# A decoder layer on one core: the recurrence of batches 2 and 3 moved into the FFN stage, with five shared PSUM banks and three tile sets

## The reference

```
x = layernorm(x + attention(x, Wqkv, bqkv, Wo, bo))        # 16 heads of 32
x = layernorm(x + wkv(w, u, k=x, v=ctx))                   # a recurrence over the 512 tokens
x = layernorm(x + ffn(x))                                  # 512 -> 2048 -> 512
# wkv: per step t, y = (A*p + E*v)/(A*q + E), then p, q, o are decayed by w and updated
# ffn: Wg = (gate_w - 128)*gate_scale, same for up and down
#      y = (silu(x Wg') * (x Wu')) Wd'
```

## Time and profile before

| | us |
|---|---|
| median of three runs | 837.01 |
| the profiled execution | 835.81 |
| its span (first to last instruction) | 834.0 |
| PE busy in the span | 743.1 |
| DVE busy | 558.8 |
| ACT busy | 408.3 |
| POOL busy | 271.2 |

### The profile page before, as it was taken

One profiled execution on the slowest core, in us unless ns is written; L12 is line 12 of the kernel. 1 busy time (PEld: TensorE's weight loads), 2 busy tenths in 40 slices (PEclk: granted clock), 3 DMA queues, 4 the chain that ended last, 5 costly groups with the idle time before them and its releaser, 6 DMA issues.

```text
span 834.0 us, 11936 instructions
## 1 busy us (share of the span) xinstructions
PE 743.1 (89%) x4256; PEld 404.1 (48%) x4256; DVE 558.8 (67%) x1217; ACT 408.3 (49%) x1000; POOL 271.2 (33%) x284
## 2 busy tenths in 40 slices
PE   5988699978889978999677598889999999999997
PEld 2555456644456545565443254434454444444443
DVE  4455545778998879998898488874774544344434
ACT  5568767777567776686846213302332034104310
POOL 2001233328341155500346515541622133103320
PEclk9999799998999989999979899999999999999999
DMA  7246494232034122141620610001000100010001
GB/s 248 62 138 217 139 215 127 89 114 65 13 89 139 44 72 77 33 117 56 133 44 1 101 51 1 1 13 39 2 1 13 38 1 1 14 38 1 1 13 38
DMA packets 44331, 54.17 MB, mean 65 GB/s; under 512 B 4720, under 2 KB 33648, under 8 KB 44272
## 3 DMA queue, kind: packets, MB, share of 16 engines
q1 hardware_dynamic: 41008, 47.11, 18.0%
q0 software_dynamic: 3264, 6.29, 4.4%
HBM read 47.10 MB, written 12.58 MB: 72 GB/s over the span
## 4 chain that ended last, share of the span: by engine, by line
PE 59%; DVE 18%; issue 6%; POOL 6%; ACT 5%; DMA 3%; SPq 3%; POOLq 0%; DVEq 0%; ACTq 0%
PE psb L717 20%; PE psb L607 7%; PE psb L730 6%; PE psb L728 6%; PE psb L697 5%; PE psb L654 4%; DVE ek L1034 4%; DVE ee L946 3%; PE psb L621 2%; SPq L1270 2%; PE psb L643 2%; DMA xt<-in_xT 2%; PE psb L665 2%; PE psb L704 1%; PE psb L633 1%
## 5 line engine op out<-in xcount | busy, mean ns | idle before, releaser
L946 DVE CUSTOM_DVE_ANT_0 ee<-psb,mask,clip 128x512 f32<-128x512 f32 (+3 forms) x256 | 131.0, 530 | 54.7 <-PE psb L643 54.1
L810 ACT ACTIVATE ee<-ee,nm 128x512 f32<-128x512 f32 (+3 forms) x256 | 142.8, 559 | 32.4 <-DVE nm L946 32.1
L654 PE MATMUL psb<-ident,ee 128*128 128x128 f32 x640 | 108.5, 288 | 25.9 <-ACT ee L821 25.7
L821 ACT ACTIVATE ee<-psb 128x512 f32<-128x512 f32 (+1 forms) x192 | 100.0, 521 | 56.4 <-PE psb L654 56.1
L1212 POOL TENSOR_TENSOR hl<-hf,hh 128x512 f16<-128x512 f32 x64 | 77.5, 1211 | 134.9 <-ACT hh L884 134.9
L884 ACT ACTIVATE hh<-hf 128x512 bf16<-128x512 f32 x64 | 40.4, 632 | 144.1 <-DVE hf L1059 144.1
L717 PE MATMUL psb<-x2h,wg 128*128 128x512 f16 x256 | 99.5, 389 | 6.6 <-DVE th L1049 5.9
L654 PEld LDWEIGHTS psb<-ident,ee 128*128 128x128 f32 x640 | 76.3, 147 | 54.2 <-ACT ee L821 34.5
L717 PE MATMUL psb<-x2l,wg 128*128 128x512 f16 x256 | 99.7, 390 | 0.0
L730 PE MATMUL psb<-wd,hl 128*128 128x512 f16 x256 | 97.0, 379 | 2.3 <-POOL hl L1212 2.3
L717 PE MATMUL psb<-x2h,wu 128*128 128x512 f16 x256 | 97.5, 381 | 0.0
(11 more groups left out here) (106 smaller groups left out, 1236.3 us busy)
## 6 DMA issues: line engine op xcount, KB each, us to landing
qs<-parts SPq DMA_DIRECT2D x64, 128.0 KB, 2.7
ks<-parts SPq DMA_DIRECT2D x64, 128.0 KB, 2.9
parts<-qhl SPq DMA_DIRECT2D x16, 256.0 KB, 2.1
parts<-khl SPq DMA_DIRECT2D x16, 256.0 KB, 2.1
x<-in_x SPq DMA_DIRECT2D x4, 1024.0 KB, 7.8
ct<-in_ctxT SPq DMA_DIRECT2D x4, 1024.0 KB, 6.2
out<-x SPq DMA_DIRECT2D x16, 256.0 KB, 2.0
xt<-in_xT SPq DMA_DIRECT2D x14, 256.0 KB, 4.0
```

The source lines that it names most:

```text
L654: mm = e.transpose(PSB[:, bk, o:o + P], E[H % 3][:, EOFF[i] + j * P:EOFF[i] + (j + 1) * P], IDENT[:])
L810: e.activation(dst, dst, ACT.Exp, bias=NM[:, n % 4, col:col + 1], scale=-1.0, accum_out=DEN[:, n % 4, col:col + 1]).then_inc(sem("exp"), 1)
L821: e.activation(ET[h][:, base:base + width], PSB[:, bank["turn", H, item], 0:width], ACT.Copy).then_inc(sem("et"), 1)
L946: e.tensor_tensor_reduce(E[H % 3][:, EOFF[i]:EOFF[i] + w], PSB[:, bank["score", H, i], 0:w], MASK[:, S - w:S], -SC, CLIP[:, i:i + 1], ALU. ...
```

## The change

Of the recurrence of batch 2, three pieces go from attention groups 14 and 15 to iterations 4, 11 and 14 of FFN batch 0, the fourth to iteration 1 of batch 1. Batch 3's four go to iterations 8, 12 and 15 of batch 1 and 2 of batch 2. `yt` of batch 2 moves to iterations 4 to 7 of batch 1, `yt` of batch 3 to 6 to 9 of batch 2; the load of the context for batch 3 follows `yt` of batch 2 as before. Batch 3's Wo comes after iterations 5 to 8 of batch 0 instead of ahead of iteration 4. The zero-point pass of the down weights stands in iterations 8 to 15 instead of 4 to 11, `x2t` in 12 to 15 instead of 10 to 13. Gate and up take the bank of banks 0 to 4 that is emptied first in the list, and `th`/`hf` tiles come in three sets from iteration 4 on (two before).

```diff
-X2IT, YTIT = (10, 11, 12, 13), (6, 7, 8, 9)
+X2IT, WOIT = (12, 13, 14, 15), 5
+WKV2, WKV3 = ((0, 4), (0, 11), (0, 14), (1, 1)), ((1, 8), (1, 12), (1, 15), (2, 2))
+YT2, YT3 = [(1, 4 + t) for t in range(4)], [(2, 6 + t) for t in range(4)]
+FBANK = (0, 1, 2, 3, 4)
...
-        for u in gu_parts(b, it, ((0, 2), (1, 3))):
+        for u in gu_parts(b, it, (FBANK, FBANK)):
...
-        for c, (g, slot) in enumerate(WKVS):
-            at(m + g, slot, "wkv", b, c)
         if b < B - 2:
+            for c, (g, slot) in enumerate(WKVS):
+                at(m + g, slot, "wkv", b, c)
...
-    wk3 = [lambda c=c: wkv(B - 1, c) for c in range(T)]
-    for it in range(IT):
-        if it >= EARLY:
-            gu(0, it)
+    ffn = {}
+    for c in range(T):
+        ffn.setdefault(WKV2[c], []).append(lambda c=c: wkv(2, c))
+        ffn.setdefault(WKV3[c], []).append(lambda c=c: wkv(3, c))
+        ffn.setdefault(YT2[c], []).append(lambda c=c: yt(2, c))
+        ffn.setdefault(YT3[c], []).append(lambda c=c: yt(3, c))
+        for b in (1, 2, 3):
+            ffn.setdefault((b - 1, X2IT[c]), []).append(lambda b=b, c=c: x2t(b, c))
+    for it in range(EARLY, IT):
+        gu(0, it)
         tick()
-        if it < 4:
-            for u in wo3[3 * it:3 * it + 3]:
+        if it - WOIT in range(T):
+            for u in wo3[3 * (it - WOIT):][:3]:
                 u()
-            tick()
-            yt(B - 2, it)
-        if it in (5, 9, 13):
-            wk3.pop(0)()
-        if 4 <= it < 12:
-            add("zero", "wd", 2 * it - 8)
-            add("zero", "wd", 2 * it - 7)
-        if it in X2IT:
-            x2t(1, X2IT.index(it))
+        if it >= 8:
+            add("zero", "wd", 2 * it - 16)
+            add("zero", "wd", 2 * it - 15)
+        for u in ffn.get((0, it), ()):
+            u()
         tick()
...
                 gu(b, it)
                 tick()
-                if b == 1 and it == 1:
-                    wk3.pop(0)()
+                for u in ffn.get((b, it), ()):
+                    u()
                 tick()
-                if b == 1 and it in YTIT:
-                    yt(B - 1, YTIT.index(it))
-                if b + 1 < B and it in X2IT:
-                    x2t(b + 1, X2IT.index(it))
...
+    def ring(b, it):
+        z = b * IT + it
+        return RINGS[z % 2 if z < EARLY else (z - EARLY) % 3]
+    def ring_had(b, it):
+        z = b * IT + it
+        return max([k + 1 for k in range(z) if ring(0, k) is ring(b, it)], default=0)
...
-            if z >= 2:
-                act.wait_ge(sem("hf"), z - 1)
+            if ring_had(b, it):
+                act.wait_ge(sem("hf"), ring_had(b, it))
```

More of the change, by code:

```diff
@@ L502, in build @@
         wg = sb(f, "wg", [P, T, I], F16)
-        TH, HF = sb(f, "th", [P, 2, S], F32), sb(f, "hf", [P, 2, S], F32)
+        RINGS = [(sb(f, f"th{k}", [P, S], F32), sb(f, f"hf{k}", [P, S], F32)) for k in (0, 1)]
         wd = sb(f, "wd", [P, IT, D], F16)
@@ L506, in build @@
         HS = [(sb(f, f"hh{it}", [P, S], BF16), sb(f, f"hl{it}", [P, S], F16)) for it in range(IT)]
-        sb(f, "pad1", [P, 19 * 256], F32)
+        sb(f, "pad1", [P, 15 * 256], F32)
+        RINGS.append((sb(f, "th2", [P, S], F32), sb(f, "hf2", [P, S], F32)))
         YS = sb(f, "ys", [P, 2, D], F32)
@@ L867, in th @@
         def th(b, it):
-            z = b * IT + it
             act.wait_ge(*by("gate", b, it))
             act.wait_ge(sem("small"), 4)
-            if z >= 2:
-                act.wait_ge(sem("hf"), z - 1)
-            e.activation(TH[:, it % 2, :], PSB[:, bank["gate", b, it], :], ACT.Tanh,
+            if ring_had(b, it):
+                act.wait_ge(sem("hf"), ring_had(b, it))
+            e.activation(ring(b, it)[0][:], PSB[:, bank["gate", b, it], :], ACT.Tanh,
                          scale=GT[:, it:it + 1]).then_inc(sem("th"), 1)
@@ L883, in hh @@
                 act.wait_ge(*by("et", NHG - 1, 2))
-            e.activation(HS[it][0][:], HF[:, it % 2, :], ACT.Copy).then_inc(sem("hh"), 1)
+            e.activation(HS[it][0][:], ring(b, it)[1][:], ACT.Copy).then_inc(sem("hh"), 1)
         for name, *a in tt.order:
@@ L1048, in aa @@
             dve.wait_ge(*by("th", b, it))
-            e.scalar_tensor_tensor(out=TH[:, it % 2, :], in0=TH[:, it % 2, :], scalar=1.0,
+            th = ring(b, it)[0]
+            e.scalar_tensor_tensor(out=th[:], in0=th[:], scalar=1.0,
                                    in1=PSB[:, bank["gate", b, it], :], op0=ALU.add,
@@ L1053, in hf @@
         def hf(b, it):
-            z = b * IT + it
+            th, half = ring(b, it)
             dve.wait_ge(*by("aa", b, it))
             dve.wait_ge(*by("up", b, it))
-            if z >= 2:
-                dve.wait_ge(sem("hl"), z - 1)
-            e.scalar_tensor_tensor(out=HF[:, it % 2, :], in0=TH[:, it % 2, :], scalar=CC[:, it:it + 1],
+            if ring_had(b, it):
+                dve.wait_ge(sem("hl"), ring_had(b, it))
+            e.scalar_tensor_tensor(out=half[:], in0=th[:], scalar=CC[:, it:it + 1],
                                    in1=PSB[:, bank["up", b, it], :], op0=ALU.mult, op1=ALU.mult).then_inc(sem("hf"), 1)
@@ L1211, in hl @@
             pool.wait_ge(*by("hh", b, it))
-            e.tensor_tensor(HS[it][1][:], HF[:, it % 2, :], HS[it][0][:], ALU.subtract).then_inc(sem("hl"), 1)
+            e.tensor_tensor(HS[it][1][:], ring(b, it)[1][:], HS[it][0][:], ALU.subtract).then_inc(sem("hl"), 1)
         e.memset(NT[:], -10000.0).then_inc(sem("nt"), 1)
```

## The result

The changed kernel takes 846.95 us (median of 4 runs, 842.85 to 849.13) against 836.87 for the kernel before: 10.1 us slower, ratio 1.0116, 95% interval 1.0073 to 1.0159. The forecast was 816.7. In its profiled execution the span is 847.3 us against 834.0.

The account below looks back on a forecast made before the run. DVE was taken to bound groups 14 and 15 through batch 2's recurrence, PE the FFN stage. Gains of 15.5 us (attention) and 4.8 (FFN, 16.8 less 12.0) sum to 20.3: 837.0 to 816.7 us, range 806 to 828.

Parts of the forecast that it names:

- The first y product: FFN batch 0: hl(0, 15) as late as before, behind an exp on ACT waiting for `y2`; loss 2.0 us (0 to 4).
- Attention groups: Without recurrence, group 14 gains 3.5 us, group 15 5.4 and 5.1, the finish 1.5; sum 15.5, between about 7 and 19.
- The loads' cost: Group 14: gate weights' loads go out together near 398 us beside re-stacking of group 15's score inputs; 0, at worst 3.
- Rival (a): Attention groups are paced by their chain, gaining 7.5 us instead of 15.5: 824.7 us; chance 0.17.
- ol: FFN batch 0: PE waits for hf and `ol` before Wo, behind iteration 5's products; loss 1.5 us (0 to 3.2).
- Iterations 11 to 15: FFN batch 0: five banks shrink one gate-product stall to 1.3 us, the other vanishes; with clock, loss 2.3 us (0 to 6).
- yt(2, 0): Batch 1, iteration 4: PE idles 4.0 us for the POOL product, plus 1.7 for the clock; loss 5.7 us (4 to 6).
- Batch 3 has no such wait: Batch 2: no wait at `yt` of batch 3, since (2, 2) to (2, 6) has eight ticks; priced at none.
- PE's own work: From 471.6 us on: the same matmuls in both kernels, some later, so no difference was counted.
- Rival (c): Port shared by DVE and POOL: two zero pairs meet a piece, stalling PE by 3.8 us in batch 0; 820.5, chance 0.09.
- Rival (d): FFN stage: each of eight recurrence pieces stalls PE, 4.3 us each, making it slower: 848.3 us; chance 0.05 with its like.
- The signs named ahead: Wrong if group 15 over 40 us, gate-product idle over 2 in batches 1 or 2, or wait before yt(2, 0) below 2.

Follow-up runs that it names:

- experiments 1 to 3: Zero passes of the down weights: in iterations 4 to 11 of changed kernel, 828.51 us; ahead of its gate products, 833.22; in 8 to 15 of kernel before, 846.04.
- experiment 1: Changed kernel with the zero passes of the down weights back in iterations 4 to 11 of FFN batch 0: 828.51 us, ratio 0.9892.
- experiments 6 and 11: Five banks and three tile sets alone put into the kernel before, 840.41 us; taken out of the 814.40 us kernel again, 814.44 us.
- the best kernel: Changed kernel with early zero passes, recurrence pieces, `yt` and `x2t` re-placed, gate loads spaced, last `ol` two ticks earlier: 814.40 us, ratio 0.9705.
- experiment 4: Changed kernel with two recurrence pieces of batch 2 after iterations 9 and 13 of batch 0 instead of 11 and 14: 842.49 us, ratio 1.0059.
- experiment 5: Changed kernel with the last recurrence piece of batch 2 after iteration 0 of batch 1 instead of 1: 840.80 us, ratio 1.0037.

## Why the prediction was wrong

- **The first y product** is the step that failed. Of the 30.4 us by which the FFN stage missed (a gain of 4.8 forecast, a loss of 25.6 measured) it is 14.1, the largest term. It was priced at 2.0 us, as a wait for hl(0, 15). The zero passes were in the sum as DVE time only ("0.5 to 2.5" an iteration), although the change moves them from iterations 4 to 11 to 8 to 15. The question who waits for the last of them was not put. It cost 13.3 + 2.8 = 16.1 us; experiments 1 to 3 show that it is this wait, and that it makes the old kernel 8.3 us slower by itself. The wait is 9.65 us there and 13.3 here; what makes the difference was not separated. Mended alone (experiment 1) it gives 828.51, still 12 us above the forecast. The terms below are the others.
- **Attention groups**: forecast 15.5, measured 15.9 in the profile, by other amounts. Group 15 gained 17.3 against 5.4 + 5.1, the finish nothing against 1.5, and group 14, forecast at +3.5, lost 1.4. The loads' cost of "0, at worst 3" was 6.1 us. That they "go out together" was seen; that SP's put of k, issued in the midst of them, would land 5 us later was not priced.
- **Rival (a)**, a pace set by the chain, did not come: PE is busy 16.55 of 17.5 us in the long part of group 15.
- **ol**: forecast 1.5, measured 2.35, and the clock did fall after it (0.57 for 4.0 us, 1.7 us more).
- **Iterations 11 to 15**: forecast 2.3, measured 0 (45.3 of 45.3 us busy). The forecast owed a part of its low price to the depth; two other schedules are the same without it (experiments 6 and 11). Here DVE was late as feared, but the loss fell on the first y product and not on gate products.
- **yt(2, 0)**: found at the right place and released by the POOL product, but 6.7 us for 4.0, from a backlog of 2.7 that was left out, and 2.6 us for 1.7 at the lower clock (0.50 for 5.3 us).
- **"Batch 3 has no such wait"** was wrong: 3.1 us, and 1.3 at the lower clock. Eight ticks suffice for the order in the list, not for the time that POOL and DVE take.
- **First y product of batch 1**: 4.0 us for x2l and 1.4 at the lower clock, not forecast. This x2l stands on DVE behind a reciprocal of piece (3, 1) that waits 1.08 us for POOL.
- **PE's own work** behind 471.6 us was put down as the same in both kernels, but the four `x1t` of batch 2 moved there too: 112 of these 128x128 transpositions (L716) from 459.3 us on, 96 (L704) from 471.6 before. The prediction took their 1.6 us out of the attention groups and put them in nowhere; at 0.43 us for four they are 1.7.
- **Rival (c)**, the shared port. The pairs in iterations 12 and 15, beside POOL's recurrence work, took 2.46 and 2.45 us, those in 13 and 14 took 1.39 and 1.38, and those in 8 to 11 took 0.49. This agrees with what the Trainium skill says ("SBUF — State Buffer", "Who interferes with whom"), that such a DVE operation and a POOL operation take turns. No gate product was stalled by it, as the rival had it, but the last pair ends PE's longest wait, so about 2 us of its 3.8 are in the 13.3. Late pairs on DVE are also in the 4.4 us of backlog.
- **Rival (d)** has the right side by the wrong mechanism: no piece stalls PE at gate products. The losses behind 459.3 us, 4.1 (ol) + 16.1 + 9.3 (yt(2, 0) with its clock) + 5.4 + 4.4 = 39.3, stand against 16.8 before: 22.5 more of the 25.6 measured (388.0 against 362.4 us). Of the remaining 3.1 us, 1.7 are the moved `x1t` and 0.4 two short waits; 1 us I have not placed. Slower was given 0.05.
- **The signs named ahead** did not show the miss. Group 15 fell under 40 us, no gate product of batches 1 and 2 waited 2 us, the wait before yt(2, 0) was above 2, and the gate product of iteration 4 came 60 us after group 14's start. Only DVE above 70% in the first slots of groups 14 and 15 was against them. None of them looked at the y products.

That the best kernel lands at 814.4, near the forecast of 816.7, is no merit of it: it has other places for over a dozen pieces. It does show that the recurrence can lie in the FFN stage at a gain, and that the places chosen for it lost that gain. What stays open: why the same wait was followed by 1.3 us lost at the lower clock in one kernel and by 2.8 in another, which is most of what experiments 4 and 5 gave beyond the waits they shortened.

## What to carry to other kernels

When a series of small operations is moved, look for who waits for its last one, and where that one now stands in its engine's order; the sum of their durations is not the price. A wait on "all of them" at the head of a stage turns the last member into the critical one. Extra buffers did not help in the two schedules tried here, where an engine's sum of work over the stretch was late. And signs to look for should cover every stage that the change touches, not only those where a cost is expected. A load that leaves its queue earlier because other work was moved away can delay a transfer that PE needs.

## What the runs showed of the hardware

- A transfer of 256 KB issued from SP at 402.6 us took 10.2 us until its reload could start, beside four 512 KB loads from POOL's queue; 5.2 us with one such load beside it in the kernel before.
- The granted clock fell after PE idle times of 2.17, 3.02 and 2.35 us, not after one of 2.33 in a y product (clock 1.00 after it). After 13.3 us idle it was 0.66 over 8.2 us in the changed kernel, 0.84 over 8.4 us in that of experiment 5. In the kernel of experiment 4 it did not fall after 1.66 us.
- A pair of zero passes that took 2.46 us behind one order took 0.43 behind another.
- Identical work ahead of group 14 took from 395.2 to 399.4 us in fourteen profiles.
